# B and C of a selective-scan step: one matmul of 32 columns and a spread through DRAM in place of two matmuls of 128 columns

## The reference

```python
xz = x @ in_proj_w.T
xs, z = jnp.split(xz, 2, axis=-1)          # 128 channels each
xs = silu(conv(xs, 4 taps) + conv_b)
dbc = xs @ x_proj_w.T                       # 16 columns for dt, 16 for B, 16 for C
dt = softplus(dbc[..., :16] @ dt_proj_w.T + dt_proj_b)
Bm, Cm = dbc[..., 16:32], dbc[..., 32:]
dA = exp(dt[..., None] * A)                 # 128 channels x 16 states
dBu = dt[..., None] * Bm[:, :, None, :] * xs[..., None]
hs = scan(h -> dA * h + dBu, along the tokens)
y = einsum('blds,bls->bld', hs, Cm) + xs * D
y = (y * silu(z)) @ out_proj_w.T
```

## Time and profile before

| what | value |
|---|---|
| median of 3 runs | 5216.6 us (5200.36 to 5223.23) |
| the profiled execution | 5213.57 us |
| its span, first to last instruction | 5211.8 us |
| mean granted TensorE clock | 0.937 of 2.4 GHz |
| first scan to last scan | 274.4 to 5074.3 us |
| PE busy | 84% |
| VectorE busy | 77% |
| GpSimd busy | 75% |
| ScalarE busy | 64% |
| mean share of the 16 DMA engines busy | 51.5% for the hardware queue |

### The profile page before, as it was taken

One profiled execution on the slowest core, in us unless ns is written; L12 is line 12 of the kernel. 1 busy time (PEld: TensorE's weight loads), 2 busy tenths in 40 slices (PEclk: granted clock), 3 DMA queues, 4 the chain that ended last, 5 costly groups with the idle time before them and its releaser, 6 DMA issues. The chain is left out here.

```text
span 5211.8 us, 70837 instructions
## 1 busy us (share of the span) xinstructions
PE 4357.3 (84%) x21206; PEld 1771.7 (34%) x21206; DVE 4025.3 (77%) x6073; ACT 3334.8 (64%) x5405; POOL 3922.9 (75%) x4937
## 2 busy tenths in 40 slices
PE   3577788888888888888889888789888888888887
PEld 1233333333333333333333333333333333332332
DVE  2278887888877887888878888788878788788771
ACT  1255566767666766676767676667666676676665
POOL 1277787888877887888878888788878888788772
PEclk9588999999999998999999999899999999999997
DMA  2365564555555654555545555455555555554420
GB/s 66 72 148 141 134 140 114 138 131 136 125 118 118 140 132 106 135 136 129 133 113 134 131 133 127 109 137 136 130 116 131 128 135 127 115 117 106 98 62 5
DMA packets 255558, 623.33 MB, mean 120 GB/s; under 512 B 105268, under 2 KB 170676, under 8 KB 255028
## 3 DMA queue, kind: packets, MB, share of 16 engines
q1 hardware_dynamic: 255156, 618.60, 51.5%
HBM read 540.85 MB, written 77.65 MB: 119 GB/s over the span
## 5 line engine op out<-in xcount | busy, mean ns | idle before, releaser
L1193 POOL TENSOR_TENSOR hc<-hs,cb 128x448 f32<-128x448 f32 x1792 | 2030.5, 1136 | 751.6 <-DVE hs L1030 726.9
L1030 DVE TENSOR_TENSOR_SCAN hs<-dtb,state,ps 128x448 f32<-128x448 f32 x1792 | 2047.4, 1143 | 105.8 <-issue 1.8
L1020 DVE TENSOR_TENSOR ps<-ps,bb 128x448 f32<-128x448 f32 x1792 | 1098.7, 613 | 443.9 <-PE ps L687 437.9
L865 ACT ACTIVATE dtb<-dtb,decay 128x448 f32<-128x448 f32 x1792 | 1086.2, 657 | 198.4 <-DMA dtb<-dt_scratch 193.5
L687 PE MATMUL ps<-dux,pick 128*128 128x448 bf16 x3584 | 1049.1, 374 | 164.6 <-DVE hs L1030 102.5
L907 ACT ACTIVATE hg<-ps,be 128x448 f32<-128x448 f32 x896 | 520.1, 631 | 430.5 <-PE ps L751 429.0
L687 PE MATMUL ps<-duz,pick 128*128 128x448 bf16 x1792 | 649.2, 362 | 0.0
L751 PE MATMUL ps<-xn,we 64*128 64x448 f32 x1792 | 583.3, 621 | 53.5 <-ACT hg L907 53.0
L687 PEld LDWEIGHTS ps<-dux,pick 128*128 128x128 bf16 x3584 | 264.6, 99 | 865.4 <-issue 527.8
L734 PE MATMUL ps<-h,w 96*128 96x448 bf16 x896 | 313.0, 385 | 212.5 <-ACT rz L896 86.3
L699 PE MATMUL ps<-hc,gather 128*32 128x448 f32 x3584 | 454.2, 580 | 8.7 <-POOL hc L1193 8.4
(11 more groups left out here) (175 smaller groups left out, 6277.2 us busy)
## 6 DMA issues: line engine op xcount, KB each, us to landing
dtb<-dt_scratch SPq DMA_DIRECT2D x448, 896.0 KB, 6.6
slab<-h_scratch SPq DMA_DIRECT2D x168, 290.0 KB, 8.1
dt_scratch<-sp SPq DMA_DIRECT2D x112, 224.0 KB, 2.0
h_scratch<-h2p SPq DMA_DIRECT2D x168, 112.0 KB
h<-h_scratch SPq DMA_DIRECT2D x56, 336.0 KB, 4.1
h_scratch<-h1s SPq DMA_DIRECT2D x56, 232.0 KB, 3.9
xw<-xn_scratch SPq DMA_DIRECT2D x112, 112.8 KB, 2.6
xw<-xn_scratch SPq DMA_DIRECT2D x112, 112.5 KB, 2.7
```

Source lines behind the costliest of these rows:

```text
L865: A.activation(a, a, ACT.Exp, scale=decay[k % 2][:, i:i + 1]).then_inc(a_ok, 1)
L1020: V.tensor_tensor(bank, bank, bb[:, k % 2, :], ALU.mult).then_inc(bu_ok, 1)
L1030: V.tensor_tensor_scan(rev(hs[:, n % RH, :], d), rev(dtb[i // 4][:, i % 4, :], d), rev(bank, d), state[:, d, i:i + 1], ALU.mult, ALU.add). ...
L1193: P_.tensor_tensor(hc[:, n % 8, :], hs[:, n % RH, :], cb[:, k % 2, :], ALU.mult).then_inc(hc_ok, 1)
```

## The change

The weights keep their 32 columns (wbc: B and C side by side). At slot 2 PE makes both with one matmul into 32 rows of the bank MB. ScalarE copies 32 x 448 values to the new tile bc at slot 3 (`copy_bc`). SyncE writes bc to DRAM at slot 3 (`put_bc`, 56 KB) and reads it back at slots 6 and 8 (`spread_bc`), B into bb and C into cb, each row repeated eight times (224 KB each). VectorE and GpSimd wait for these transfers in place of ScalarE. Four small copies in the preparation go. Cut to its core:

```diff
-        wbb = [sb(f"wbb{d}", [DI, 128]) for d in range(2)]
-        wcc = [sb(f"wcc{d}", [DI, 128]) for d in range(2)]
+        wbc = [sb(f"wbc{d}", [DI, 2 * DS]) for d in range(2)]
...
+        bc = sb("bc", [2 * DS, CH])
...
+        bc_dram = nc.dram_tensor("bc_scratch", (2, 2 * DS, CH), F32, kind="Internal").ap()
...
-                    for out, at in ((wbb[d], 0), (wcc[d], DS)):
-                        then(V.tensor_copy(out[:, :].rearrange("p (s e) -> p s e", e=8),
-                                           wbc[d][:, at:at + DS].unsqueeze(2).to_broadcast([DI, DS, 8])))
...
-                    MISC += [(DS * k + 4, "bb", k + 1), (DS * k + 6, "cc", k + 1)]
+                    MISC += [(DS * k + 2, "bc", k + 1)]
...
+                    def put_bc(kk):
+                        sp_.wait_ge(m_act, by_act("bc", kk))
+                        sp_.dma_start(bc_dram[kk % 2], bc[:, :]).then_inc(bc_out, 16)
+
+                    def spread_bc(kk, half):
+                        sp_.wait_ge(bc_out, 16 * (n2(kk) + 1))
+                        if run and kk >= 2:
+                            sp_.wait_ge(hc_ok if half else bu_ok, DS * (kk - 1))
+                        out, landed = ((bb, bb_in), (cb, cb_in))[half]
+                        src = bc_dram[kk % 2, DS * half:DS * half + DS, :]
+                        sp_.dma_start(out[:, kk % 2, :], src.unsqueeze(1).to_broadcast([DS, 8, CH]))\
+                           .then_inc(landed[kk % 2], 16)
...
+                            if i == 3 and second_half(k):
+                                put_bc(k + 1)
                             if i == 5 and second_half(k):
                                 put_dt(k + 1)
+                            if i in (6, 8) and second_half(k):
+                                spread_bc(k + 1, (6, 8).index(i))
...
-                        if what == "bb":
-                            last = MM(out[:, 0:CH], wbb[of % 2][:, :], u[:, of % 2, :], start=True, stop=True)
-                        elif what == "cc":
-                            last = MM(out[:, 0:CH], wcc[of % 2][:, :], u[:, of % 2, :], start=True, stop=True)
+                        if what == "bc":
+                            last = MM(out[0:2 * DS, 0:CH], wbc[of % 2][:, :], u[:, of % 2, :], start=True, stop=True)
...
+                    def copy_bc(kk):
+                        act.wait_ge(m_ps, misc_made("bc", kk))
+                        after(bc_out, 16 * n2(kk))
+                        A.activation(bc[:, :], ps[MB][0:2 * DS, 0:CH], ACT.Copy).then_inc(m_act, 1)
...
-                            if i == 5 and second_half(k):
-                                copy_bb(k + 1)
-                            if i == 7 and second_half(k):
-                                copy_cc(k + 1)
+                            if i == 3 and second_half(k):
+                                copy_bc(k + 1)
...
-                            dve.wait_ge(m_act, by_act("bb", k))
+                            dve.wait_ge(bb_in[k % 2], 16 * nth(k))
...
-                            pool.wait_ge(m_act, by_act("cc", k))
+                            pool.wait_ge(cb_in[k % 2], 16 * nth(k))
```

More of the change, by code:

```diff
@@ L192, in build @@
         rows = [early[:, 1408 + 128 * d:1536 + 128 * d] for d in range(2)]
-        wbc = [early[:, 1664 + 2 * DS * d:1664 + 2 * DS * d + 2 * DS] for d in range(2)]
         bnv = early[:, 1728:1810]
@@ L376, in build @@
         xw_in = [sem("xw_in0"), sem("xw_in1")]
+        bc_out, bb_in, cb_in = sem("bc_out"), [sem("bb_in0"), sem("bb_in1")], [sem("cb_in0"), sem("cb_in1")]
         dtb_in = [sem(f"dtb_in{j}") for j in range(4)]
@@ L424, in n2, with nth @@
                 return kk - 1 if run else kk - STEPS
+            def nth(kk):
+                return (kk + 1) // 2 if run else 1
             def xn_of(kk):
@@ L667, in _ @@
                     if nxt:
+                        sp_.wait_ge(bb_in[0], 16 * nth(STEPS))
+                        sp_.wait_ge(cb_in[0], 16 * nth(STEPS))
                         for j in range(3):
```

## The result

The changed kernel takes 5698.6 us (median of 4 runs, 5663.4 to 5720.8) against 5218.7 for the kernel before: a ratio of 1.092, interval 1.086 to 1.098. It is slower by 480 us; the forecast was 5460, at most 5600. The profiled execution has a span of 5701.4 us and a mean granted clock of 0.885, against 5211.8 and 0.937.

What follows compares the result with a forecast made beforehand. No engine is full: DVE's unbroken slots 0 to 6 bound odd steps, POOL and the dt transfer even ones. 77 + 103 + 69 - 1 = 248 us on 5213.6 gave 5461.6, rounded to 5460 us, range 5280 to 5600.

Steps and rivals of the forecast that it cites:

- Fold wait: Odd steps, slot 2: PE's new matmul waits 2.4 us for the fold's reader, making DVE 1.5 us late; 77 us.
- SyncE's queue: Even steps: put_bc ahead of the third put makes dt and ACT's first decay 2.1 us late; 103 us.
- Clock: Longer PE waits bring 1.2 GHz; half of one 2.8 us stretch per pair of steps, 69 us.
- Relief: One PE matmul (102 us) and one ACT copy (60 us) fewer gain nothing, since both engines wait anyway.
- (a): Rival: the waits come but the clock holds; 5393 us, chance 0.22.
- (b): Rival: only the fold wait counts, the queue's lateness is taken up; 5290 us, chance 0.13.
- (c): Rival: no change, as DVE's slots 3 to 6 and the queue have slack; 5214 us, chance 0.07.
- (d): Rival: faster, as PE decides slots 4 to 8 of even steps; 5071 us, chance 0.10.
- (e): Rival: late spreads make DVE wait for bb, or low clock holds most of each step; above 5600 us, chance 0.06.
- L791's wait, 50 times: Sign: in odd steps PE waits about 2.4 us before the new matmul for L1125, some 50 times.
- L1029's new wait: Sign: in odd steps DVE shows a new wait of over 1 us for L687 at slots 3 and 4.
- Slot 8's wait 3.2: Sign: in even steps PE's wait for POOL at slot 8 goes from 1.40 to 3.2 us.

Runs made afterwards that it cites:

- fill_even: Changed kernel with 8 small matmuls ahead of even steps' slot 8 wait for routed tokens and 8 ahead of slot 14's transposes; 5735.8 us, ratio 1.103.
- no_c: Kernel before with the matmul of C, its eviction and its wait left out, B's tile read in place of C's; 5244.9 us, ratio 1.004.
- both_off: Changed kernel with the matmul in slot 4, copied in slot 5, put behind dt, spread in slots 10 and 12, all steps; 5219.6 us, ratio 1.003.
- square_18: Changed kernel with ScalarE's square of a chunk and what follows it one slot later; 5702.1 us, ratio 1.097.
- fill_odd_2: Changed kernel with small filler matmuls in odd steps, 11 ahead of the fold wait and 9 ahead of slot 10's transposes; 5571.5 us, ratio 1.071.
- part_late: Changed kernel with GpSimd's third part of dt times u moved from slot 6 to slot 8; 5531.1 us, ratio 1.062.
- before_mean_16: Kernel before with VectorE's mean and centring of a chunk one slot later; 5485.7 us, ratio 1.048.
- mean_16_square_18: Changed kernel with VectorE's centring one slot later and ScalarE's square with what follows it one slot later; 5530.6 us, ratio 1.062.
- both_and_fill: Changed kernel with VectorE's centring and ScalarE's square one slot later, plus 11 small matmuls ahead of odd steps' fold wait; 5449.8 us, ratio 1.046.

## Why the prediction was wrong

The direction and both waits were right, the size was not: forecast 248 us, measured 480.

- *Fold wait, 77 us.* As a wait it was well sized: 2.4 forecast and 2.55 measured, 1.5 forecast and 1.7 measured as what it costs at full clock. The step that failed is "The 1.5 us fall into DVE's unbroken stretch. 51 folds x 1.5", which took lateness for a plain sum. It had two consequences that no term held: the low clock right behind the wait, and VectorE's centring pushed from GpSimd's small operations on to its long ones. All that hangs on the wait is 7.0 us an odd step; undone alone it gives 331 us (5698.6 to 5367.8; 310 by the ratios).
- *SyncE's queue, 103 us.* The mechanism held; it measured 148 alone. dt's put is 2.6 us late and the decay 2.9, not 2.1. Missing were 0.9 us from "In even steps slot 2 has no fold before it; the 0.91 moved there makes slot 3's L687 at most 0.1 us late: nothing": true for L687, but the up matmuls and so ScalarE's split, which releases the third put, went 0.9 us later too. SyncE's own wait for dt ahead of the put, 0.48 us (2414.15 and 1.25 to 2415.88), took some of it back.
- *Clock, 69 us.* Put in even steps, half a stretch each. In even steps of the changed kernel it is worth at most 0.3 us a step beside the late dt (fill_even); in odd ones, where none was put, the fillers gave 2.75 us a step back, and step 51 shows 4.85.
- *Relief, 0.* Right, and for the reason given: TensorE only waits longer. It is even a small loss, 0.4% in no_c (and 0.3% in both_off, which has the transfers too), and low clock stands behind the longer wait.
- *Rivals.* (a) fell: the clock fell behind waits of 2.55 and 2.14 us. It leaned on the Trainium skill (TensorE: Matmul & The Clock Gate, HAM oscillation), whose gaps are longer than these; the trace decides against it here. (b), (c) and (d) fell with the result. (e) named waits for bb and low clock for most of a step; bb is never waited for, and the clock is low 19% of the time, so above 5600 was right for a reason that it only half had.
- *Sums and readings.* That "the steps repeat nearly to 0.1 us" does not hold: before, even steps took 41.7 to 48.2 us and odd ones 37.4 to 47.7, as the three of the earlier trace rows already say. 2454.7 less 2453.50 is 1.2, not 1.25; the third put comes by its own terms 2.0 us late, not 2.1; and the terms given for the upper end of the range add up to 5578, not 5600. None of this changes the outcome. The section of the Trainium skill cited for bytes / 436e9 (DMA: Bandwidth & Descriptors, Anatomy of one DMA) is on transfers that GpSimd issues; here SyncE issues them, and the sum rightly went by rows 10.
- *Signs.* L791's wait, 50 times: right. L1029's new wait: right, larger. ACT's wait for dtb 300: 271.5. Slot 8's wait 3.2: 2.0, since TensorE loses 1.1 us earlier to an eviction.

Open: about 1.4 us of slots 11 and 12 in fill_odd_2's odd steps, with 1.9 us of low clock left in slots 9 to 11, wasn't separated; nor why fill_even's odd steps grew, nor why the clock falls behind some waits of 1.9 us and not behind others, and in square_18 behind shorter ones.

## What to carry to other kernels

A wait placed in front of the busiest engine can cost its length, then the work behind it at half clock, then whatever its lateness collides with; here 1.8 us of wait became 7.0. Look for the next run of GpSimd operations under a two-input operation of VectorE before calling a shift harmless. What counts is when a held-up operation ends and who waits for it, not its length alone: L1077 took 1471 ns in the kernel before and 364 after, and that bought little. Work taken from an engine that waits anyway can be a loss, as in no_c, where 1.9 us of low clock followed the longer wait. And try a small put with a consumer waiting on it ahead of bulk DMAs in the same queue: it gave 0.7% in the kernel before and nothing on top of both_off.

## What the runs showed that was not expected

- VectorE's operation on two inputs in SBUF (112 x 256, f32) takes 0.42 us alone. Begun under a row of long GpSimd operations it took 1.67, 1.76 and 2.56 us (part_late, before_mean_16, the changed kernel), and ended each time 0.27 to 0.29 us behind the last long one, in step 51 past two that each began after it. The small copy that comes next did not hold it up but took longer itself, 0.38 us where most such copies take 0.19, and in before_mean_16 GpSimd goes on behind the copy when VectorE is done:

```profile
2597.53 1.76 DVE L1069 SCALAR_TENSOR_TENSOR tmp<-stat,res 112x256 f32<-112x256 f32 x1
```

```profile
2598.96 0.38 POOL L1198 COPY state<-hs 128x2 f32<-128x2 f32 x1
2599.30 2.27 POOL L1193 TENSOR_TENSOR hc<-hs,cb 128x448 f32<-128x448 f32 x2
```

  So it is not the end of GpSimd's whole run that lets VectorE in. GpSimd's 112 x 32 cast, too, took 0.47 us instead of 0.21 where VectorE's had begun just before. The Trainium skill (SBUF — State Buffer, Who interferes with whom) has it that such an operation and a GpSimd operation that reads SBUF hold a shared port one against the other, whoever is first; the trace agrees, and adds that GpSimd's next long operation went ahead of a VectorE operation that had waited since the one before. Why the copy did not is open.
- Eleven matmuls that compute nothing, 2.4 us in a wait of 2.55, made the kernel 81 us faster (mean_16_square_18 and both_and_fill).
- Means over the 37 even steps: a put of dt lands in 4.4 us behind three bulk DMAs and in 2.0 ahead of them.
